# A fused attention and feed-forward block: the first feed-forward product with its rows on partitions

## What is computed

```
h = layer_norm(xn, ln1_g, ln1_b)
h = h @ ternary(w1).T + b1            # 256 -> 1024
h = gelu(h)
h = layer_norm(h, ln2_g, ln2_b)       # over 1024
out = h @ ternary(w2).T + b2          # 1024 -> 256
```

## Time and profile before

| | us |
|---|---|
| median of 3 runs | 1508.13 (1507.6 to 1510.3) |
| the profiled execution | 1508.56 |
| its span, first to last instruction | 1506.8 |

### The profile page before, as it was taken

The page is one execution under the profiler, slowest core; times in us unless marked ns, Lnnn a source line. Parts: engine busy times, 40 slices in busy tenths (PEclk is TensorE's granted clock), DMA queues, the critical chain, the costliest instruction groups (busy, mean ns, idle before and its releaser), DMA issues.

```text
span 1506.8 us, 25898 instructions
## 1 busy us (share of the span) xinstructions
PE 1465.9 (97%) x9914; PEld 783.7 (52%) x9914; DVE 898.0 (60%) x1716; ACT 1205.8 (80%) x1269; POOL 97.4 (6%) x193
## 2 busy tenths in 40 slices
PE   7899999999999999999999999999999999999997
PEld 6354555455554555555555545545555455554544
DVE  5537664576555765458654685547765576555654
ACT  2688788888888887888878878788788888888884
POOL 2000100010000100001000010000100001000000
PEclk9899999999999999999999999999999999999999
DMA  6442043510524105241063401443033510425100
GB/s 202 110 128 69 1 102 96 140 57 16 126 68 129 57 15 154 76 103 47 17 167 89 122 1 54 129 128 83 1 94 103 140 57 15 119 66 138 29 1 29
DMA packets 67436, 123.49 MB, mean 82 GB/s; under 512 B 12784, under 2 KB 14448, under 8 KB 66288
## 3 DMA queue, kind: packets, MB, share of 16 engines
q1 hardware_dynamic: 67312, 121.83, 29.6%
HBM read 79.84 MB, written 41.94 MB: 81 GB/s over the span
## 4 chain that ended last, share of the span: by engine, by line
issue 93%; POOLq 6%; POOL 1%; DVE 0%; DVEq 0%
POOLq L534 3%; POOL rs L520 1%; POOLq L510 1%; POOLq L526 1%; POOLq L519 0%; POOLq L528 0%; POOLq L524 0%; POOLq L522 0%; POOLq L219 0%; DVE part L772 0%; DVEq L219 0%; POOL ident L500 0%; POOL rat L529 0%; POOLq L504 0%; POOLq L503 0%
## 5 line engine op out<-in xcount | busy, mean ns | idle before, releaser
L562 ACT ACTIVATE attn<-scores 128x1024 f32<-128x1024 f32 x1024 | 991.3, 1023 | 228.4 <-PE scores L930 224.3
L949 PE MATMUL outs<-attn,V 128*32 128x512 f32 x4096 | 494.3, 600 | 0.0
L930 PE MATMUL scores<-QS,KS 64*128 64x512 f32 x2048 | 389.1, 453 | 13.0 <-ACT attn L562 7.5
L930 PEld LDWEIGHTS scores<-QS,KS 64*128 64x128 f32 x2048 | 163.1, 185 | 306.2 <-ACT attn L562 241.5
L949 PEld LDWEIGHTS outs<-attn,V 128*32 128x32 f32 x4096 | 107.2, 109 | 235.7 <-issue 235.6
L822 DVE TENSOR_TENSOR tmp<-fill,l2g 128x512 f32<-128x512 f32 x128 | 88.5, 692 | 89.8 <-PE fill L1014 81.8
L805 DVE SCALAR_TENSOR_TENSOR hid<-fill,ratq,fb1b 128x512 f32<-128x512 f32 x128 | 96.1, 751 | 77.0 <-PE fill L1005 72.1
L1021 PE MATMUL fill<-Wq,hgh 128*128 128x256 f32 x512 | 130.2, 292 | 1.8 <-DVE hgl L829 1.1
L987 PE MATMUL fill<-xp,W1h 128*128 128x512 f32 x384 | 128.2, 415 | 0.0
L1021 PE MATMUL fill<-Wq,hgl 128*128 128x256 f32 x512 | 124.9, 282 | 0.0
L1021 PEld LDWEIGHTS fill<-Wq,hgh 128*128 128x128 f32 x512 | 97.3, 190 | 19.0 <-issue 14.9
(11 more groups left out here) (112 smaller groups left out, 1339.0 us busy)
## 6 DMA issues: line engine op xcount, KB each, us to landing
QS<-q_scratch SPq DMA_DIRECT2D x256, 128.0 KB, 3.2
k_scratch<-kst SPq DMA_DIRECT2D x64, 256.0 KB
q_scratch<-qst SPq DMA_DIRECT2D x64, 256.0 KB
KS<-k_scratch SPq DMA_DIRECT2D x128, 128.0 KB, 3.2
KS<-k_scratch SPq DMA_DIRECT2D x256, 64.0 KB, 3.4
xin<-in_x SPq DMA_DIRECT2D x8, 1024.0 KB, 5.0
out_dram<-part SPq DMA_DIRECT2D x16, 512.0 KB, 2.7
w1raw<-in_W SPq DMA_DIRECT2D x1, 1024.0 KB, 7.2
```

Source lines behind the costliest of these rows:

```text
L562: nc.scalar.activation(attn_of(g)[:, 2 * hf:2 * hf + 2, :], SP[:, 2 * hf:2 * hf + 2, :], ACT.Silu).then_inc(s_silu, 1)
L930: ins = mm(SP[:, j, :], KS[rows, pair, t * P:(t + 1) * P], QS[rows, pair - c * PPC, h * HALF:(h + 1) * HALF], start=True, stop=True)
L949: ins = mm(OP[32 * j:32 * j + 32, g // RUN % 2, :], V[:, t, c * HPC // 2 + j, o * DH:o * DH + 2 * DH], attn_of(g)[:, n, :], start=(o == 0 ...
```

## The change

`f1` is turned: step `f1.h.c` computes 128 hidden features on partitions for 512 tokens (half h), as eight matmuls of 256 columns with `Wq1` as the weights. DVE adds the bias as a per-partition scalar. The scale by the ratio of rstds moves ahead, into `y`: the ratio goes to DRAM and comes back as a row broadcast over partitions (`rrow`). `g`, `ln2` and `nrm2` go. `hg.t.r` multiplies the gelu'd block by `ln2_g` and splits it as `g` did, without PE. For each pair of tiles DVE sums over the eight feature blocks (`sum.i`), POOL sums the squares in 15 instructions, and `ts.i` brings both across partitions with four matmuls of two columns; DVE and POOL make variance, rstd and `nm2 = -mean*rstd` (per token), which are applied when `f2` is evacuated, by two DVE instructions, the first of them with `gwb`, a row made in setup. `x` of the next batch is loaded after `px`. The table is laid out anew; in batch 0 the steps of rounds 0 to 2 are all done in round 2.

```diff
--- before.py
+++ after.py
...
+SETUP_ROUNDS = {0: (), 1: (), 2: (0, 1, 2)}
-FILLERS = ("zt", "a", "u", "f1", "g", "f2", "xt", "k", "q", "v")
+FILLERS = ("zt", "a", "u", "f1", "ts", "f2", "xt", "k", "q", "v")
-    for g in (2 * n, 2 * n + 1):
+    rounds = (n,) if b else SETUP_ROUNDS.get(n, (n,))
+    for g in (g for r in rounds for g in (2 * r, 2 * r + 1)):
...
+    ratio = nc.dram_tensor("ratio", [P, T], F32, kind="Internal").ap()
...
-        hid45 = at("hid45", [P, 2, HID], F32, vraw_at)
+        hid67_at = top[0]
         hid67 = sb("hid67", [P, 2, HID], F32)
+        hid47 = at("hid47", [P, 2, HC, PAIR], F32, vraw_at)
...
-        hid03 = at("hid03", [P, 4, HID], F32, xh_at)
+        hid03 = at("hid03", [P, 2, HC, PAIR], F32, xh_at)
...
+        gwb = sb("gwb", [P, D], F32)
+        acc = sb("acc", [P, 2, PAIR], F32)
+        sq = sb("sq", [P, PAIR], F32)
+        fb1c = sb("fb1c", [P, HC], F32)
+        mean_of = sb("mean_of", [P, 2], F32)
...
+        y01 = at("y01", [P, 2, 2, DC, PAIR], F32R, hid67_at)
+        y2 = at("y2", [P, 2, DC, PAIR], F32R, kst_at)
+        rrow = at("rrow", [P, SEQ], F32, hg_at + 4 * 2 * HALF)
+        fb1r = at("fb1r", [HC, P], F32, hg_at)
+        bcastg = at("bcastg", [P, HC, P], F32, hid67_at)
...
+            return (y01[:, 0, :, :, :], y01[:, 1, :, :, :], y2, yT)[i]
...
+            def write_ratio(x):
+
+                if x:
+                    sp.wait_ge(s_row, 16 * x)
+                sp.wait_ge(s_rat, x + 1)
+                sp.dma_start(ratio, rat[:, :]).then_inc(s_ratw, 16)
+
+            def load_ratio(x):
+
+                if x:
+                    wait_evacuated(sp, x - 1, ("f2", T - 1))
+                sp.wait_ge(s_ratw, 16 * (x + 1))
+                sp.dma_start(rrow[:, :], ratio.rearrange("p t -> (p t)").partition_broadcast(P)).then_inc(s_row, 16)
...
+                    load_ratio(b)
...
+                    if h == 0 and b < NB - 1:
+
+                        sp.wait_ge(s_px, b + 1)
+                        load_x(b + 1)
...
-                    wait_evacuated(sp, b, ("f1", T - 3, 1))
-                    load_x(b + 1)
+                    write_ratio(b + 1)
...
-                elif kind == "ln2":
+                elif kind == "sum":
+                    i = a[0]
+                    pool.wait_ge(s_gelu, NP * x + i // 2 * 2 + 2)
+                    if x or i:
+                        wait_filled(pool, *((x, ("ts", i - 1)) if i else (x - 1, ("ts", NP - 1))))
+                    rows = hid_pair(i)
+                    nc.gpsimd.tensor_tensor(acc[:, 1, :], rows[:, 0, :], rows[:, 0, :], ALU.mult)
+                    for c in range(1, HC):
+                        nc.gpsimd.tensor_tensor(sq[:, :], rows[:, c, :], rows[:, c, :], ALU.mult)
+                        pool.drain()
+                        ins = nc.gpsimd.tensor_tensor(acc[:, 1, :], acc[:, 1, :], sq[:, :], ALU.add)
+                        pool.drain()
+                    ins.then_inc(s_sq, 1)
+                elif kind == "ts":
+                    ts = slice(2 * a[0], 2 * a[0] + 2)
                     pool.wait_ge(s_mv2, NP * x + a[0] + 1)
-                    rsqrt(rs2[:, :], mv2[:, :, 1], rp2[:, :], 2, s_rs2)
+                    nc.gpsimd.tensor_tensor(rs2[:, ts], var2[:, ts], mhalf[:, 0:2], ALU.pow)
+                    pool.drain()
+                    nc.gpsimd.tensor_tensor(nm2[:, ts], rs2[:, ts], negm[:, ts], ALU.mult).then_inc(s_rs2, 1)
...
-                    wait_evacuated(act, x, ("f1", 2 * i + 1, 1))
-                    rows = hid_pair(i)
+                    wait_evacuated(act, x, ("f1", i // 2, i % 2 * 4 + 3))
+                    rows = hid_half(i // 2)[:, :, i % 2 * 4:i % 2 * 4 + 4, :]
...
+                V_.tensor_scalar(l1g[:, :], l1g[:, :], cq[:, 0:1], None, ALU.mult)
+                V_.tensor_scalar(l1b[:, :], l1b[:, :], cq[:, 0:1], None, ALU.mult)
+                V_.tensor_scalar(l2g[:, :], l2g[:, :], cq[:, 1:2], None, ALU.mult)
+                dve.drain()
+                for n in range(DC + HC):
+                    v = bet[:, n:n + 1] if n < DC else l2b[:, n - DC:n - DC + 1]
+                    V_.tensor_scalar(bcasts[:, n, :], ones[:, :], v, None, ALU.mult)
+                for n in range(HC):
+                    ins = V_.tensor_scalar(bcastg[:, n, :], ones[:, :], l2g[:, n:n + 1], None, ALU.mult)
                 ins.then_inc(s_bc, 1)
...
+                V_.tensor_copy(gwb[:, :], FP[:, 1, D:2 * D]).then_inc(s_setup, 1)
...
+                dve.wait_ge(s_cmm, 3)
+                V_.tensor_copy(fb1c[:, :], FP[:, 0, 0:HC]).then_inc(s_setup, 1)
...
+                    row = rrow[:, :].rearrange("q (p t) -> q t p", t=T)[:, 2 * i:2 * i + 2, :]
                     for c in range(DC):
-                        V_.tensor_scalar(y[:, c, :], y[:, c, :], l1g[:, c:c + 1], None, ALU.mult)
+                        yc = y[:, c, :].rearrange("p (j n) -> p j n", j=2)
+                        V_.scalar_tensor_tensor(out=yc, in0=yc, scalar=l1g[:, c:c + 1], in1=row,
+                                                op0=ALU.mult, op1=ALU.mult)
                     dve.drain()
...
                 elif kind == "f1":
-                    t, hf = a
-                    if me == ("f1", T // 2, 0):
+                    h, c = a
+                    if me == ("f1", 1, 0):
 
                         dve.wait_ge(s_v, 2 * x + 2)
                     wait_filled(dve, x, me)
-                    cols = slice(hf * HALF, (hf + 1) * HALF)
-                    V_.scalar_tensor_tensor(out=hid_of(t)[:, cols], in0=FP[:, k, :], scalar=ratq[:, t:t + 1],
-                                            in1=fb1b[:, cols], op0=ALU.mult, op1=ALU.add).then_inc(s_evac[k], 1)
-                elif kind == "ln2":
-                    i = a[0]
-                    dve.wait_ge(s_gelu, NP * x + i + 1)
-                    stats([[hid_of(2 * i + j)[:, n * HALF:(n + 1) * HALF] for n in range(2)] for j in range(2)],
-                          st2, mv2, s_mv2)
-                elif kind == "nrm2":
-                    i = a[0]
-                    dve.wait_ge(s_rs2, NP * x + i + 1)
-                    for j in range(2):
-                        row = hid_of(2 * i + j)
-                        ins = V_.tensor_scalar(row, row, mv2[:, j, 0:1], rs2[:, j:j + 1], ALU.subtract, ALU.mult)
-                    ins.then_inc(s_hn, 1)
-                elif kind == "g":
+                    V_.tensor_scalar(hid_half(h)[:, :, c, :], FP[:, k, :].rearrange("p (i n) -> p i n", i=2),
+                                     fb1c[:, c:c + 1], None, ALU.add).then_inc(s_evac[k], 1)
+                elif kind == "sum":
+                    i = a[0]
+                    dve.wait_ge(s_gelu, NP * x + i // 2 * 2 + 2)
+                    V_.tensor_reduce(acc[:, 0, :], hid_pair(i).rearrange("p c n -> p n c"), mybir.AxisListType.X,
+                                     ALU.add).then_inc(s_sum, 1)
+                elif kind == "ts":
+                    i = a[0]
+                    ts = slice(2 * i, 2 * i + 2)
+                    wait_filled(dve, x, me)
+                    sums = FP[:, k, 0:8].rearrange("p (n j u) -> p n j u", n=2, j=2)
+                    V_.tensor_scalar(negm[:, ts], sums[:, 0, :, 0], -1.0, None, ALU.mult)
+                    dve.drain()
+                    V_.tensor_tensor(var2[:, ts], negm[:, ts], negm[:, ts], ALU.mult)
+                    dve.drain()
+                    V_.tensor_tensor(var2[:, ts], sums[:, 1, :, 0], var2[:, ts], ALU.subtract).then_inc(s_evac[k], 1)
+                    dve.drain()
+                    V_.tensor_scalar(var2[:, ts], var2[:, ts], 0.0, EPS, ALU.max, ALU.add).then_inc(s_mv2, 1)
+                elif kind == "hg":
                     t, r = a
-                    wait_filled(dve, x, me)
+                    if r == 0:
+                        dve.wait_ge(s_gelu, NP * x + t // 4 * 2 + 2)
+                        if t:
+                            wait_filled(dve, x, ("f2", t - 1))
                     V_.tensor_tensor(tmp[:, :].rearrange("p (c n) -> p c n", n=P),
-                                     FP[:, k, :].rearrange("p (c n) -> p c n", n=P),
-                                     l2g[:, 4 * r:4 * r + 4].unsqueeze(2).broadcast_to([P, 4, P]),
-                                     ALU.mult).then_inc(s_evac[k], 1)
+                                     hid_pair(t // 2)[:, 4 * r:4 * r + 4, t % 2 * P:(t % 2 + 1) * P],
+                                     l2g[:, 4 * r:4 * r + 4].unsqueeze(2).broadcast_to([P, 4, P]), ALU.mult)
                     dve.drain()
                     V_.tensor_copy(hgh[:, r, :], tmp[:, :])
                     dve.drain()
                     V_.tensor_tensor(hgl[:, r, :], tmp[:, :], hgh[:, r, :].bitcast(F32), ALU.subtract).then_inc(s_hg, 1)
                 elif kind == "f2":
                     t = a[0]
+                    dve.wait_ge(s_rs2, NP * x + t // 2 + 1)
+                    V_.scalar_tensor_tensor(out=part[:, t, :], in0=gwb[:, :], scalar=nm2[:, t:t + 1],
```

(59 more changed lines are left out.)

215 lines of the change are left out of this document (112 added, 103 removed).

## The result

The changed kernel takes **1554.8 us** (median of 4 runs, 1553.8 to 1559.7), beside 1508.0 for the kernel before on the same chip: ratio **1.031**, 95% interval 1.0297 to 1.0322. It is slower by 47 us. The forecast was 1501, the range ended at 1536. The profiled execution took 1554.4 with a span of 1552.3, against 1508.56 and 1506.8.

What follows compares the result with a forecast made beforehand. PE was taken as the bound. Six batches at -2.9, +3.4 and +0.4 for first and last made -13.6 us; 6.4 back for DVE-POOL meetings left -7.2 on a 1506.8 span: 1501 us, range 1489 to 1536.

Steps and rivals of the forecast that it cites:

- The rule of rounds: PE's rounds: each lasts the longer of 4.82 us and 3.20 plus its PE steps.
- its table: New round lengths of a batch, summed: 178.1 us, 2.9 less than 181.0.
- The floor: Rounds with few PE steps last 4.82 us, as the two groups' SiLUs and scores wait for each other.
- The place where the cover would be used up: Round 12: DVE finishes f1.1.1's evacuation at 13.0, PE wants the bank for f1.1.3 at 12.9.
- The sum's term: DVE's sum over 2048 elements: taken as 2.3 us, upper end 4.6 for the strided read.
- Rival 4: The sum takes 4.6 us, putting DVE 2.3 behind in round 12: 3 to 4 a batch, 1527 us; chance 0.06.
- half-waits: Each hg instruction on DVE waits half a POOL instruction: 3 x 0.25, 0.8 late a batch, 6.4 us in all.
- The squares: POOL's chain of 15 instructions at 0.5 us each, 9.6 in all, 12.6 with meetings, in time for ts.
- rival 1: POOL's squares, at 0.75 an instruction with whole waits, cost PE more than the transposes did: 1536 us; chance 0.33.
- Setup, +8 forecast: Setup and first batch: bcasts product 3.55 more, columns 5.8 replacing 3.5, k.1.0 1.5, a wait 0.8: about +8 us.
- The last batch, +0.4 forecast: Last batch: fewer rounds fall for lack of next-batch steps, and a.0 falls on f2.5: +0.4 us.
- rival 3: ts takes 1.9 us, lengthening rounds 14, 17, 22 and 27 by 0.8, 3.1 a batch: 1518 us; chance 0.07.

Runs made afterwards that it cites:

- e3: Changed kernel with the sum's reduction reading neighbours in memory and POOL squaring only the first slice: 1506.9 us, ratio 0.9993.
- e1: Changed kernel with the sum's reduction reading eight neighbours in memory instead of elements 1024 bytes apart: 1522.3 us, ratio 1.009.
- e2: Changed kernel with POOL squaring only the first slice, the reduction left as it was: 1550.0 us, ratio 1.026.
- e6: Changed kernel with DVE's sum done as four two-operand additions in place of one reduction, same result: 1554.9 us, ratio 1.030.
- e11: Changed kernel with e4's order, xn.3 ahead of q.0.0, sum.3 in round 23, bias columns by DMA, other setup records spread over rounds 3 and 4: 1520.5 us.
- e4: Changed kernel with f1.1.1's evacuation ahead of hg.0.0 and sum.0, and hg.0.1 behind those of f1.1.2 and f1.1.3: 1537.3 us, ratio 1.020.
- e5: Changed kernel without the setup's 24 one-column matmuls for the first product's bias, one meaningless product instead: 1546.2 us, ratio 1.024.

## Why the prediction was wrong

**Right.** The rule of rounds, and its table: 178.1 forecast, 178.3 in e3. That the sums agree to 0.2 is partly luck: round 13 took 7.43 there for 6.5, with 0.6 of waiting, and rounds 14, 15, 22 and 27 were shorter than forecast by 0.8 together. The floor did not move (4.82 in every kernel). `f1` is 1.04 (701.79 to 702.85 is 1.06), rounds 12, 14 and 15 are near the forecast (10.50 and, in e3, 10.35 for 10.5; 4.82 for 5.1), and `ts` took 704.79 - 703.85 = 0.94, forecast 1.1, lower end 0.9. The place where the cover would be used up was named: `f1.1.3` behind `hg.0.0` and `sum.0`. Counted as in the prediction, with `gelu.1` done at 8.1 (686.59), PE wanted the bank at 13.0 (forecast 12.9), and DVE had emptied it at 15.3 (693.75), where the forecast had 13.0 and 0.8 more for meetings: the 1.5 in between is the reduction. Rounds 12 to 17 last 47.3 us, over the 43 that was set as the mark of a wrong forecast.

**The step that failed first: "with no row for the stride I take 2.3".** The sum's term measured 3.85, near the upper end of 4.6, and at a place that the working itself called just used up. Rival 4 had the mechanism with a chance of 0.06, and its price: 3 to 4 a batch, in e1 3.9. The Trainium skill's page SBUF — State Buffer (Door 1: The DMA port swizzle) says that each access that leaves a 16-byte line pays; e1 agrees in direction, 2.29 against 3.85 for the same count of elements, a factor of 1.7. Of two ends, the one nearest to a row was taken, but that row (`px`) had another walk.

**Where DVE and POOL meet.** The forecast charged half-waits, 0.8 a batch; measured, from e1 to e3, 2.1 a batch. In the chain of round 13 it was about right: `hg.0.0` took 2.46 (686.59 to 689.05) against 2.0 without the squares (e3, 0.69 + 0.43 + 0.69 and the gaps). What was not priced are rounds 16 to 21, where DVE's work for `xt` and `xn` follows `hg`. That no meeting was charged to the reduction was right. The Trainium skill's page SBUF — State Buffer (Who interferes with whom) says that `tensor_reduce` never contends on this chip and that two SBUF inputs do; e2 and e6 agree with both, by 3.83 against 3.85 and 1.05 against 0.69. The cast of `hg`, with one input, was slowed as well (575 against 441), as the forecast had it.

**The squares.** Forecast 0.5 an instruction, measured 0.61 and 0.73 undisturbed and 0.72 and 0.81 in the mean: the term was near the upper end of 0.8, as rival 1 and its estimate had it. The chain took 13.3, forecast 9.6 with 3 for meetings. But rival 1's price did not follow: in the changed kernel no `ts` waits for POOL, since DVE has already held PE up and PE comes to `ts.0` 3.9 after the chain's end. Where PE comes earlier, in e1, `ts` does wait, 2.8 in all, and in e6 9.3.

**The half clock.** No term had it. A wait of 2.3 us cost more than 2.3: rounds 13 and 14 together are 3.3 longer than in e3, where 0.6 of waiting is left; so of the 3.3 about 1.7 is idle time (18.6 less 4.8, over eight). The other 1.6 is put down to the clock: e1, with the squares but without the half clock there, is 3.1 shorter in these rounds, of which 1.5 is idle time (18.6 less 6.7, over eight).

**Setup, +8 forecast, +12.4 measured in round 2.** The second product was right (3.54 for 3.55). The columns were 48 records at 0.12, 5.8: they measured 0.85 a column of six records, 0.14 each, and the last three 1.46, in all 8.8. `k.1.0` was 1.5 and took 2.85 at half clock. These two are 4.4 over the forecast. With the 3.4 that was forecast for batch 0 and the 6.2 by which every batch exceeds the table (184.3 - 178.1), they make 14.0 of its +15.2; about 1 us is left open.

**The last batch, +0.4 forecast, +9.5 measured.** Missing was DVE's chain ahead of the `zt` of this batch. PE and DVE there:

```profile
1506.05 0.38 PE L1108 MATMUL fill<-Wq,hgh 128*128 128x256 f32 x1 [2.69 <-DVE st L824]
```

```profile
1500.05 3.81 DVE L884 TENSOR_REDUCE acc<-hid 128x256 f32<-128x2048 f32 x1
...
1505.24 0.76 DVE L824 BATCH_NORM_STATS2 st<-fill 128x6 f32<-128x256 f32 x2
```

`sum.3` and `hg.5` stand ahead of the statistics that empty the bank for `f2.5`; round 26 is 10.98 us, in e3 6.72, which is close to the rule's length (3.20 + 2.08 + 1.55) for `f2.5` with an `a` beside it. In e11, with `sum.3` moved ahead, it is 6.99. Of the 4.3, 2.69 is the wait; the clock was at half from 1507.4 on. Rounds 13 and 14 are another 3.3 and round 16 0.8, both against e3. The remaining 1.2 is what e3's batch 7 has over the kernel before (2.8) without the 1.6 of its last round, which a half clock at 1484.3 made 6.25 and which is 4.63 in the changed kernel and in the one before. The forecast had 0.4 for it.

**The sum.** Of the 53.8 us between forecast and measurement, batches 1 to 6 hold 6 x (184.4 - 178.1 - 0.8) = 33, batch 0 11, batch 7 8, and about 1 lies outside them. The forecast's case and rival 1 were the wrong pair: the true case was rival 4's mechanism at about 1 us a reduction, and the terms for meetings, squares and setup, all too small as well, added to it. One sum among the rivals was wrong in itself: rival 3's 3.1 a batch are 25 us on the forecast, 1526 and not 1518; `ts` took 0.94, so it did not matter.

## What to carry to other kernels

Price an access by its walk, not by its count of elements; where the trace has no row with that walk and the place has no slack, the range must reach the far end with a real chance. When work goes to a second engine, ask first what the neighbour does meanwhile: here its instructions with two operands in SBUF and its casts paid, and the reductions did not. And a wait of 2.3 us on PE was paid nearly twice, the second time through the clock, where waits of 0.8 (e1) and 1.6 (e4) in the same two rounds were paid once. So losses need not add: taking away the smaller one alone may win little.

## What the runs showed of the hardware

- A sum over eight slices 1024 bytes apart (128x2048 f32 into 128x256) took 3.83 to 3.85 us, over neighbours 2.29, with or without GpSimd beside it. No other step was tried.
- GpSimd's 128x256 `tensor_tensor` took 0.61 with one operand twice, 0.73 with two, and 0.14 to 0.15 between two in a chain. Beside it VectorE's 128x512 two-operand instruction went from 0.69 to 1.05 in e6's sum, and its cast, with one operand, from 0.43 to 0.68.
- TensorE's granted clock went from 2.4 to 1.2 GHz for 3.4 us at 695.0, after idle times of 0.56, 0.42 and 2.29 us. In the setup it fell at 67.0, for 10.2 us, in a chain of one-column matmuls that had run without a gap since 62.89; in e5, without these, it fell at 72.3, for 3.4 us. Why it falls in such a chain is not shown.
- One-column f32 matmuls cost 0.14 a record at full clock and 0.24 at half, so a column of six is 0.85 or 1.46. Without the two that bring in the bias it was 0.12 a record (e11, 16 in 1.9).
